# A decoder layer in one kernel: the cross attention's output product goes from slot 14 to slot 12, with the second norm's statistics behind it

## What is computed

```python
x = _layernorm(x + attn(x, Wq, Wk, Wv))                 # 16 heads, k and v shared
x = _layernorm(x + xattn(x, ctx, ctx, mask, W1, b1, W2, b2))
    # softmax(proj(x) @ proj(ctx).T * scale + mask) @ ctx
x = _layernorm(x + ffn(x, Wg, W1, b1, Wo, bo))          # top 2 of 8 experts
# _layernorm(x) = (x - mean) / sqrt(var + eps), no weights
```

## Time and profile before

| | us |
|---|---|
| median of 3 runs | 1473.22 |
| lowest and highest | 1471.83, 1475.22 |
| the profiled execution | 1475.48 |
| its span in the trace | 1472.9 |
| `attention` in it, roughly | 0 to 846 |
| `experts` in it, roughly | 846 to 1473 |

### The profile page before, as it was taken

How to read it: one execution, slowest core, us unless ns; L and a number is a source line. 1 busy time by engine, 2 the same in 40 slices (tenths; PEclk the granted TensorE clock), 3 DMA queues, 4 the chain that set the end, 5 groups by cost and what they waited for, 6 DMA issues and landing times. The chain is left out here.

```text
span 1472.9 us, 29966 instructions
## 1 busy us (share of the span) xinstructions
PE 1276.2 (87%) x7668; PEld 899.1 (61%) x7669; DVE 1136.1 (77%) x3110; ACT 755.9 (51%) x1743; POOL 656.9 (45%) x1018
## 2 busy tenths in 40 slices
PE   6888999999999999999987307999999999968886
PEld 4443555555555555555544206888888888858876
DVE  1455788888888888888864387888888888859998
ACT  1125677777777777777775242223223322314444
POOL 1011244454544444545444472343334333447886
PEclk9998999999999999999997558999999999989999
DMA  4436456656646656655636522334433443369995
GB/s 101 106 61 101 80 104 132 127 117 133 122 120 128 128 116 122 129 120 117 122 107 234 197 81 84 130 130 133 137 131 130 133 137 130 130 247 322 336 334 198
DMA packets 171822, 211.67 MB, mean 144 GB/s; under 512 B 20048, under 2 KB 143056, under 8 KB 167632
## 3 DMA queue, kind: packets, MB, share of 16 engines
q1 hardware_dynamic: 147808, 143.92, 40.9%
q0 software_dynamic: 17680, 55.28, 10.1%
q10 hardware_dynamic: 6240, 11.34, 2.2%
HBM read 124.81 MB, written 84.89 MB: 142 GB/s over the span
## 5 line engine op out<-in xcount | busy, mean ns | idle before, releaser
L853 DVE TENSOR_REDUCE negmax<-psS 128x2 f32<-128x512 f32 x512 | 349.2, 686 | 100.1 <-PE psS L625 94.4
L755 ACT ACTIVATE probs<-psT 128x512 f32<-128x512 f32 x512 | 303.4, 598 | 171.7 <-PE psT L635 165.1
L1331 ACT ACTIVATE sig<-hb 128x512 f32<-128x512 f32 x136 | 86.1, 633 | 286.9 <-DVE hb L1414 279.8
L625 PE MATMUL psS<-kstack,qstack 96*128 96x256 bf16 x1024 | 195.4, 273 | 33.8 <-DVE kstack L949 15.3
L635 PE MATMUL psT<-qstack,kstack 99*128 99x512 bf16 x512 | 194.9, 382 | 5.1 <-ACT probs L755 5.1
L1211 POOL DMA_INDIRECT g_rows<-g,slot x136 | 135.6, 997 | 70.7 <-issue 67.4
L625 PEld LDWEIGHTS psS<-kstack,qstack 96*128 96x128 bf16 x1024 | 92.4, 104 | 90.7 <-DVE negmax L853 34.8
L391 POOL DMA_INDIRECT lists<-x,slots x128 | 127.0, 992 | 34.2 <-issue 30.3
L523 PE MATMUL psO<-probs,vaug 128*32 128x512 f32 x1024 | 140.4, 621 | 0.9 <-ACT probs L755 0.8
L1425 DVE SCALAR_TENSOR_TENSOR g<-g,xe,sig 128x512 f32<-128x512 f32 x136 | 102.2, 751 | 28.5 <-DVE g L1421 16.8
L1414 DVE TENSOR_TENSOR hb<-psHb,f_b 128x512 f32<-128x512 f32 x136 | 94.0, 691 | 37.5 <-issue 34.7
(11 more groups left out here) (201 smaller groups left out, 2950.7 us busy)
## 6 DMA issues: line engine op xcount, KB each, us to landing
rows<-g_rows SPq DMA_DIRECT2D x32, 1024.0 KB, 8.0
qstack<-q_parts SPq DMA_DIRECT2D x192, 128.0 KB
xe<-lists SPq DMA_DIRECT2D x136, 133.0 KB, 2.1
q_parts<-qpart SPq DMA_DIRECT2D x32, 384.0 KB, 2.8
sums<-x SPq DMA_DIRECT2D x32, 264.0 KB, 2.3
x2in<-sums SPq DMA_DIRECT2D x32, 264.0 KB, 4.7
xt<-in_x_t SPq DMA_DIRECT2D x32, 256.0 KB, 6.0
xres<-in_x SPq DMA_DIRECT2D x32, 256.0 KB, 3.2
```

Source lines behind the costliest of these rows:

```text
L625: last = mm(psS[:, u % 2, hh * S:(hh + 1) * S], qstack[0:KROWS, b1.s4, 2 * hp + hh, c * P:(c + 1) * P], kstack[0:KROWS, b1.s4, :], start=T ...
L755: nc.scalar.activation(probs[:, u % PT, :], psT[:, u % 2, :], ACT.Exp, scale=SELF_SCALE).then_inc(sm["exp_done"], 1)
L853: v.tensor_reduce(negmax[:, b1.s2, 2 * hp:2 * hp + 2, c], psS[:, u % 2, :].rearrange("p (h k) -> p h k", h=2), AX.X, ALU.max, negate=True) ...
```

## The change

- PE: `cross_out` goes from slot 14 to slot 12, ahead of that slot's score products. The number of matmuls is the same.
- DVE: `crec` from slot 13 to 11; `kstack`'s last part from slot 14 to 13; `y2` from slot 14 to 13, behind it; the second norm's statistics from slot 0 of the next step to slot 14, their moments from slot 1 to slot 15.
- ACT: the first of the two instructions that write `x2` goes from slot 4 to slot 3, ahead of that slot's exponentials; each half has its own increment of `x2_ready`.
- PE's transposes of `x2` in slot 5 wait for each half by itself.

```diff
@@ PE
                 if u == 5 and active(b6):
-                    wait(pe, "x2_ready", done(b6))
                     bank_read(bank_b, t, "x2_transposed")
                     for c in range(QC):
+                        wait(pe, "x2_ready", done(b6, QC, c + 1))
...
-                if u == 14 and active(b5):
+                if u == 12 and active(b5):
                     wait(pe, "cprobt_copied", done(b5))
@@ ACT
-                if u == 4 and active(b6):
+                if u == 3 and active(b6):
                     wait(act, f"x2_stored{b6.s2}", 16 * b6.half)
                     wait(act, "x2_transposed", done(b6.back(2)))
                     wait(act, f"dispatched{b6.s2}", 2 * QC * 16 * b6.half)
-                    norm(x2, rstd2, shift2, y2, b6, "rstd2_ready", "x2_ready")
+                    norm(x2, rstd2, shift2, y2, b6, "rstd2_ready", "x2_ready", range(0, 1))
+                if u == 4 and active(b6):
+                    norm(x2, rstd2, shift2, y2, b6, "rstd2_ready", "x2_ready", range(1, QC))
@@ DVE
-                if u == 0 and active(b6):
-                    wait(dve, "y2_ready", done(b6))
-                    stats(y2, stats2, b6, "stats2_ready")
...
-                if u == 1 and active(b6):
-                    moments(stats2, mv2, b6, "var2_ready")
...
-                if u == 14 and active(t):
+                if u == 13 and active(t):
                     wait(dve, "k_mid", done(t))
...
-                if u == 13 and active(b5):
+                if u == 11 and active(b5):
                     wait(dve, "cross_exp", done(b5))
...
-                if u == 14 and active(b5):
+                if u == 13 and active(b5):
                     wait(dve, "crec_ready", done(b5))
                     wait(dve, "cross_out", done(b5))
...
+                if u == 14 and active(b5):
+                    wait(dve, "y2_ready", done(b5))
+                    stats(y2, stats2, b5, "stats2_ready")
+                if u == 15 and active(b5):
+                    moments(stats2, mv2, b5, "var2_ready")
```

More of the change, by code:

```diff
@@ L671, in copy_keymap, with norm @@
                 load_context_group(act, g + 2)
-        def norm(x, rs, shift, y, b, ready, name):
+        def norm(x, rs, shift, y, b, ready, name, rows=range(QC)):
             wait(act, ready, done(b, 3))
-            for c in range(QC):
+            for c in rows:
                 last = nc.scalar.activation(x[:, b.s2, c, 0:D], y[:, b.s2, c, :], ACT.Identity,
@@ L842, in step @@
                     copy_keybias(g)
-                if u == 1 and active(b6):
-                    wait(dve, "stats2_ready", done(b6))
+                if u == 15 and active(b5):
+                    wait(dve, "stats2_ready", done(b5))
                 if u == 9 and active(b6):
```

## The result

| | before | after |
|---|---|---|
| median (us) | 1473.74 (4 runs) | 1538.38 (4 runs, 1532.97 to 1541.84) |
| ratio | | 1.0449, interval 1.0416 to 1.0483 |
| span of the profiled execution | 1472.9 | 1530.2 |
| line 612, start in step 6 and in step 31 | 187.68, 733.40 | 186.03, 794.25 |

The changed kernel is 64.6 us slower. The direction was right. The size was not: 1520.0 was forecast, and the time lies above the range's upper end of 1533.

The account below looks back on a forecast made before the run. PE's order was taken to bound most of a step, with DVE close behind. Late entry, slot 5's gain, start and drain sum to +19.1 us, 18 clock falls add +27.7; over 1473.2 that gives 1520.0 us, range 1486 to 1533.

Parts of the forecast that it names:

- What bounds the step: PE's order bounds most of a step, with three holes in it; DVE runs close behind in slots 12 to 15.
- The three holes: PE's waits in slot 5 for ACT (0.88 us), ahead of slot 0 for `kstack` (0.50), ahead of slot 13 (0.28).
- The queue on DVE: From slot 12's reduction on, `kstack` and `y2` precede slot 14's reduction, so slot 0's `psS` comes 1.04 us later.
- The late entry: PE enters the next step 1.04 us later, 27 times; less slot 5's gain and start and drain, +19.1 us.
- my 0.79 a step: Rise of the step's period: 1.04 us for slot 0's delay less 0.25 gained in slot 5.
- The price of one fall: One fall of PE's clock to the 1.2 GHz level costs 1.54 us, read from the drain of before.
- The number of falls: PE's new holes ahead of slots 15 and 0 bring the clock down in two steps in three: 18 falls, +27.7 us.
- Rival 2: Clock falls in nearly each step, 27 falls with the late entry's upper bound: 1535 us; chance 0.06.
- Start and drain: Earlier `kstack` in the first steps and slot 5's gain in the drain: -2.5 us together (0 to -4).
- Rivals 3 and 4: Rival 3: DVE catches up and the holes close, 1441.3 us, chance 0.06; rival 4: no difference, chance 0.04.
- Rival 1: The late entry alone, PE's hole leaving the clock at 1.00: 1492.3 us (1483 to 1503); chance 0.26.

Follow-up runs that it names:

- e_y2back: The changed kernel with `y2` back in slot 14, the second norm's statistics in slot 0 and moments in slot 1; 1474.71 us, ratio 1.0032.
- e_y13: The changed kernel with only the second norm's statistics and moments back in slots 0 and 1, `y2` staying in slot 13; 1539.33 us, ratio 1.0458.
- e_fill5: The changed kernel with five extra `psT` products, whose result nothing reads, in slot 0's hole; 1491.92 us, ratio 1.0148.
- e_fill1: The changed kernel with one extra `psT` product in slot 0's hole; 1521.02 us, ratio 1.0349.
- e_fill2: The changed kernel with two extra `psT` products in slot 0's hole; 1517.2 us, ratio 1.0326.
- best_b: The kernel before with `x2` in halves, `kstack` in slot 13, first norm's statistics ahead of `krest`, value projection in slot 12; 1453.62 us, on another chip 1454.93.

## Why the prediction was right and wrong

**What bounds the step: right.** The three holes were there, and the change acted on all three: `kstack` is out of the waits, slot 13's `psS` follows slot 12's by 0.44, and slot 5 is 0.22 shorter, though not closed (0.26 and 0.17 are left in the brackets).

**The queue on DVE: right, the end of it partly by luck.** Carried forward by hand from before's starts, it gave slot 0's `psS` 1.04 us later; measured 1.08. Terms off by about 0.1 cancel in that. `cross_out` took 0.87 in its new place (472.39 to 473.26) and not 0.97, so slot 12's reduction started 1.72 after slot 11's `psS` and not 1.83. Against that, slot 13's reduction to `kstack` took 0.92, the upper end of my 0.80 to 0.92, and slot 0's `psS` came 0.82 after slot 14's reduction started and not 0.74. So slot 15 came sooner, slot 0 later, and the hole between them is larger than forecast: 1.79 by starts against 1.64, 1.62 in the bracket against about 1.5. The hole ahead of slot 15 is 0.34 by starts (476.14 - 475.23 - 0.57), where 0.35 was forecast, and 0.20 in the bracket. The period was to be 22.6 without a fall and near 24.2 with one; it is 22.70 and 24.3. e_y2back and e_y13 together show that the cause is the one named, `y2` ahead of the reduction that PE needs, and that the statistics' new place costs nothing. The late entry was 19.1 us in the sum; the 25 steps show +22.1 where my 0.79 a step gives 19.8 for them. 0.88 in place of 0.79 is the 0.04 more in the queue, the 0.03 less in slot 5, and 0.02 that I can't place.

**The price of one fall: right.** 1.54 us from the drain of before; 1.55 to 1.59 measured.

**The number of falls: this step failed.** The prediction took "two steps in three, 18 falls, 18 x 1.54 = +27.7". Measured are 23 of 25 steps, three with a double fall, 26 falls by my count and 40.4 us, in the steady part alone. The row that I leaned on, a fall behind 0.80 of 2.30 us of work in the drain, said that such a hole brings the clock down. Against that row nothing stood but the 0.88 and 0.50 of before, and nothing in the trace spoke for one step in three being spared. I hedged the count where the evidence was for nearly all. The runs with one and two extra products say the same from the other side: with holes smaller than that of after the clock still fell in 19 and 15 of 25 steps. Rival 2 (falls in nearly each step, 1535) was the case that came, and had 0.06. The same forecast with 26 falls at 1.54 for those 25 steps reads 1473.2 + 19.1 + 40.0 = 1532, and the 2.3 more for the late entry makes 1535. The median of 1538.4 lies 5.4 above the profiled execution's own 1533.0.

The page "TensorE: Matmul & The Clock Gate" of the Trainium skill was used in the prediction for both sides. Its section "Why this matters for your kernels" warns of long idle gaps between bursts of matmuls, longer than any that stood here. Read as saying that shorter gaps do no harm, it would have the steady part keep its clock. Here, with a hole of 1.8 us once in a step of 24, the clock fell in 23 steps of 25, and the measurement decides. The section "A second HAM failure mode: psum-queue depth-cycling", which the prediction named, is the one that fits. It tells of a clock that swings when the matmul engine stands idle for short times between groups of matmuls that cycle through PSUM; the waits here too are for PSUM buffers.

**Start and drain.** I took -2.5 for both. The trace shows -1.7 to step 6 and -3.2 in the drain; the first is inside what one kernel differs by from run to run.

**Rivals 1, 3 and 4.** Rival 1, the late entry alone, is e_fill5: 1492.3 predicted, 1491.9 measured, but only with matmuls put into the hole. Rivals 3 and 4 needed slot 14's reduction to start 0.73 sooner than computed; it did not (slot 0's `psS` 1.08 later).

**What stays open.** All steps of after have the same holes, yet 2 of 25 kept the clock and 3 lost twice as much; with one extra product 6 kept it. What picks them wasn't tried, though the regular pattern of e_fill1, every fourth step, speaks against chance. Nor was it tried why `cross_out`'s move shortens the drain by 4 us; two falls fewer there may be most of it.

## What to carry to other kernels

On an in-order engine that also frees buffers for the matmul engine, don't ask whether a moved instruction is short, but what stands behind it: `y2`, 0.87 us, moved ahead of one reduction cost about 61 us over 32 batches, of which the queue itself (0.64 a step) explains a quarter and the matmul clock the rest.

When a change opens a stall on TensorE that is larger than any the steady part has had, and a row of the trace shows a fall behind a similar one, count a fall in nearly every step; here it was 23 of 25. If the stall can't be closed, cheap matmuls in it can pay, if they fill most of it: five products of 0.22 us a step saved about 44 us, two saved some 18. And try the parts of a change singly: this one held a gain (`x2` in halves, 0.21 us a step and 0.9% in the total) under a loss of 4.5%.

## What the runs showed that I had not expected

- **How small a hole costs the clock.** PE's idle time between slot 15's `psS` and slot 0's is the distance of their starts less the 0.44 of a frame and 0.215 for each extra product. In the steady part of each kernel:

| | idle there (us) | steps that fell, of 25 |
|---|---|---|
| before | 494.58 - 493.49 - 0.44 = 0.65 | 0 |
| e_fill5 | 485.61 - 483.37 - 0.44 - 1.08 = 0.72 | 0 |
| e_y2back | 494.62 - 493.16 - 0.44 = 1.02 | 0 |
| e_fill2 | 492.25 - 490.00 - 0.44 - 0.43 = 1.38 | 15 |
| e_fill1 | 480.07 - 477.82 - 0.44 - 0.22 = 1.59 | 19 |
| after | 478.37 - 476.14 - 0.44 = 1.79 | 23 |

In a step of 22 us, 0.36 more parts a kernel that never falls in these 25 steps from one that falls in most. The column is a sum: in the fill runs some 0.22 of it lies ahead of the extra products, so the longest single pause is 1.15 in e_fill2 against 1.02 in e_y2back. Between 1.02 and 1.38 nothing was measured. What else stands around the hole is the same in these but for `y2` and the 0.65 of before, whose slot 5 has its 0.88 besides.
- **The start scatters.** One and the same kernel (best_b, best_b_again) reached step 6 at 188.5 us in one execution and at 182.6 in another, on another chip. A gain of 5 us between two profiled executions is only safe if it shows in the length of the step.
